# One call of a cross-attention loop moved on ScalarE: the exponential of a tile ahead of the normalisation of the tile before

## What is computed

```python
qp = ctx @ Wq.T + bq ; kp = ctx @ Wk.T + bk
scores = (qp @ kp.T) * 128**-0.5 * layernorm(x)      # 512 x 512 for each batch
scores = where(mask, -inf, scores)
x = x + softmax(scores)                              # attention step, residual
xn = layernorm(x)
shared = silu(xn @ sg) * (xn @ su) @ sd              # shared expert
logits = xn @ router_w                               # 8 experts, top 2, sigmoid
x = x + shared + sum over chosen experts of ffn_e(p_e * xn)
```

## Time and profile before

| what | value |
|---|---|
| time, median of 3 runs | 365.19 us (364.84 to 365.95) |
| the profiled execution | 365.61 us, span 363.9 us |
| busy: PE, POOL, DVE, ACT | 320.0, 231.0, 208.1, 177.6 us |
| granted TensorE clock, mean | 0.958 |

### The profile page before, as it was taken

One profiled execution on the slowest core, in us unless ns is written; L12 is line 12 of the kernel. 1 busy time (PEld: TensorE's weight loads), 2 busy tenths in 40 slices (PEclk: granted clock), 3 DMA queues, 4 the chain that ended last, 5 costly groups with the idle time before them and its releaser, 6 DMA issues.

```text
span 363.9 us, 6490 instructions
## 1 busy us (share of the span) xinstructions
PE 320.0 (88%) x1627; PEld 217.8 (60%) x1627; DVE 208.1 (57%) x461; ACT 177.6 (49%) x400; POOL 231.0 (63%) x199
## 2 busy tenths in 40 slices
PE   2857999899999994648999999999999999999991
PEld 1324666576666762315776766777777777777760
DVE  0666887898998889612444444444444444444440
ACT  2467767667757645102644434444444444444430
POOL 0688999886675739948376565656555465555433
PEclk9999999999999998556999999999999999999998
DMA  7956788746646420075346466857666666575736
GB/s 186 304 203 200 222 241 239 272 145 214 221 146 196 153 86 0 0 193 165 57 92 98 83 116 118 143 95 125 113 113 117 115 119 116 91 130 86 134 36 82
DMA packets 29763, 50.61 MB, mean 139 GB/s; under 512 B 5472, under 2 KB 9312, under 8 KB 29728
## 3 DMA queue, kind: packets, MB, share of 16 engines
q0 software_dynamic: 9008, 21.66, 33.7%
q1 hardware_dynamic: 19232, 27.99, 24.3%
q10 hardware_dynamic: 1488, 0.54, 0.7%
HBM read 30.45 MB, written 19.73 MB: 138 GB/s over the span
## 4 chain that ended last, share of the span: by engine, by line
PE 48%; POOL 19%; issue 10%; ACT 7%; DMA 7%; DVE 6%; POOLq 0%; SPq 0%; DVEq 0%; ACTq 0%
PE bank L948 9%; PE bank L958 8%; PE bank L953 8%; POOL gu_lo L356 7%; PE bank L981 5%; PE bank L987 5%; PE bank L984 5%; POOL dn_lo L356 5%; PE bank L1072 4%; DMA out_rows<-y,jscatter 3%; POOL rstd L332 3%; PE bank L967 2%; ACT gu_hi L493 2%; ACT bank L488 2%; POOL pen L351 2%
## 5 line engine op out<-in xcount | busy, mean ns | idle before, releaser
L439 POOL DMA_INDIRECT out_rows<-y,jscatter x39 | 61.9, 1588 | 73.5 <-DMA out_rows<-y,jscatter 47.9
L958 PE MATMUL bank<-gu_hi,x_lo 128*128 (+1 forms) x220 | 70.9, 444 | 0.0
L948 PE MATMUL bank<-gu_hi,x_hi 128*128 (+1 forms) x220 | 62.4, 406 | 3.4 <-POOL dn_lo L356 1.4
L953 PE MATMUL bank<-gu_lo,x_bf 128*128 (+1 forms) x220 | 57.5, 384 | 0.0
L670 DVE TENSOR_TENSOR x_lo<-bank,x_hi 128x512 fp32r<-128x512 f32 x55 | 37.7, 686 | 26.4 <-ACT x_bf L507 25.3
L863 DVE SCALAR_TENSOR_TENSOR h<-bank,xg,h 128x256 f32<-128x256 f32 x39 | 18.9, 484 | 58.4 <-ACT h L594 57.0
L420 POOL DMA_INDIRECT xg<-xn_rows,jgather x39 | 41.7, 1069 | 16.1 <-issue 15.1
L514 ACT CAST h_hi<-bank 128x256 fp32r<-128x256 f32 x55 | 20.6, 374 | 60.9 <-PE bank L967 59.0
L958 PEld LDWEIGHTS bank<-gu_hi,x_lo 128*128 128x128 f32 x220 | 42.0, 191 | 12.7 <-issue 0.3
L356 POOL TENSOR_TENSOR gu_lo<-stage,gu_hi 128x1024 bf16<-128x1024 f32 x18 | 43.4, 2412 | 9.7 <-ACT gu_hi L493 9.7
L948 PEld LDWEIGHTS bank<-gu_hi,x_hi 128*128 128x128 f32 x220 | 40.5, 190 | 13.7 <-issue 3.1
(11 more groups left out here) (128 smaller groups left out, 491.5 us busy)
## 6 DMA issues: line engine op xcount, KB each, us to landing
stage<-in_L_ffn_gate_up_w SPq DMA_DIRECT2D x16, 512.0 KB, 3.8
xin<-in_x SPq DMA_DIRECT2D x16, 256.0 KB, 4.3
xn_rows<-xn SPq DMA_DIRECT2D x16, 256.0 KB, 3.8
stage<-in_L_ffn_down_w SPq DMA_DIRECT2D x8, 512.0 KB, 3.8
out_rows<-x SPq DMA_DIRECT2D x16, 256.0 KB, 4.2
out_rows<-zeros POOLq DMA_DIRECT2D x1, 1024.0 KB, 5.0
ctx_in<-in_ctx SPq DMA_DIRECT2D x1, 768.0 KB, 8.8
xg<-xn_rows,jgather POOLq DMA_INDIRECT x39
```

The source lines that it names most:

```text
L439: g.indirect_dma_start(out=out, out_offset=bass.IndirectOffsetOnAxis(ap=jscatter[:, n - TILES:n - TILES + 1], axis=0), in_=y[:, r, :], in_ ...
L948: tn.matmul(ps_g(n)[:], x_hi[:, n % TS, k, :], gu_hi[:, e, k, :], start=(k == 0), stop=False)
L953: tn.matmul(ps_g(n)[:], x_bf[:, n % TS, k, :], gu_lo[:, e, k, :], start=False, stop=False)
L958: last = tn.matmul(ps_g(n)[:], x_lo[:, n % TS, k, :], gu_hi[:, e, k, :], start=False, stop=(k == KC - 1))
```

## The change

On ACT, normal() is called one step later: in step s the exponential of tile s comes first, then the normalisation of tile s - 1, then the rest of the step. Nothing else changes, neither the semaphores nor the other engines' lists.

```diff
@@ -547,6 +547,8 @@
             for s in range(TILES):
                 j = s - LAG
                 expo(s)
+                if s:
+                    normal(s - 1)
                 if s + 1 < B:
                     projections(s + 1)
                 if s + 2 < B:
@@ -563,7 +565,6 @@
                         chosen_exp(j)
                     if s == TILES - 2:
                         late_high(EARLY)
-                    normal(s)
 
             chosen_exp(FIRST - 1)
             h_high(FIRST - 1)
```

## The result

The changed kernel takes 363.47 us (median of 9 runs, 362.2 to 364.35) against 365.31 us before (9 runs): the ratio is 0.9942, with a 95% interval of 0.9925 to 0.9958. That is 2.1 us faster by the ratio (1.5 to 2.7), where 1.8 us was forecast.

A forecast was written before the change was run, and what follows sets the result against it. POOL was taken to set steps 1 to 6, and equal POOL-ACT and TensorE loops the later ones, TensorE limiting the gain. Terms 0.34 + 1.25 + 0.15, said as 1.8 us, gave 363.4 us against the median; range 362.7 to 364.2.

The forecast's parts named there:

- The three loops of a later step: Steps 7 to 14: ACT and POOL need 5.97 us, DVE 6.30 to 6.34, TensorE 6.68 to 6.72, the longest.
- the repeated 4.62 us: TensorE's stretch L948 to L911 takes 4.62 us in later steps and in step 7 alike, so it is work, not waiting.
- the full busy row: Later steps: the matmul engine is busy 6.72 of 6.72 us, read as TensorE having no room.
- The eight later steps: Steps 7 to 14 together gain 0 to 0.3 us, taken as 0.15, since TensorE's loop limits them.
- The join: Step 7, after POOL's pace ends: L967 starts 1.25 us earlier, won once and kept by TensorE.
- The second rival: Transposes of xn hold TensorE in steps 2 to 6, so the join wins 0.5 us or less: 364.7 us; chance 0.20.
- The first steps: Steps 1 and 2: POOL's low_part comes 0.34 us earlier (bounds 0 and 0.59); steps 3 to 6 only carry it on.
- The tail: Step 15 onward: an earlier exponential gives 0 to 0.1 us, and what is won at step 15 arrives at the first gather.
- The sum: Whole kernel: 0.34 + 1.25 + 0.15 = 1.74 us, said as 1.8 with the start of the tail.
- The slower rival: Later steps lengthen if DVE's bias comes over 0.3 us later against TensorE: 367.9 us; chance 0.09.
- One sign to watch: In the changed profile, POOL's low_part still waits, longer than before.

The follow-up runs named there:

- run 6: Changed kernel with the shared expert's low part of gate and up cut to one slice of four for tiles 0 to 13; single execution 363.23 us.
- Run 5: Kernel before (old order) with the shared expert's low part of gate and up cut to one slice of four for tiles 0 to 13; single execution 367.11 us.
- run 1: Only normal() of tiles 0 to 6 moved, the other tiles in the old place, against the kernel before: 363.44 us, ratio 0.9955.
- run 2: Only normal() of tiles 7 to 14 moved, the other tiles in the old place, against the kernel before: 365.24 us, ratio 0.9993.
- run 3: Only normal() of tiles 5 to 14 moved, the other tiles in the old place, against the kernel before: 363.21 us, ratio 0.9946.
- run 4: The full change once more, all 15 normal() calls moved, against the kernel before: 362.82 us, ratio 0.9932.
- run 7: Old order with the second weight chunks in steps 0, 1, 3, 5, 7 and 9, not 0 to 5, against the kernel before: 366.43 us, ratio 1.0025.
- Run 10: Changed kernel with DVE's x_stats ahead of neg_max, so the exponential's bias comes 0.6 us later; steps 8 to 13 took 6.76 to 6.77 us, no kernel time given.

## Why the prediction was right

*The three loops of a later step* were forecast at 5.97 us (ACT and POOL), 6.30 to 6.34 (DVE) and 6.68 to 6.72 (TensorE). The runs show each by itself: nmr(6) to nmr(7) in the changed kernel is 5.97 us; the steps of run 6 are 6.35; those of the changed kernel 6.69, with TensorE alone in the chain. Run 5 shows that the first of them was real as well. The reason I gave for TensorE (the repeated 4.62 us) holds; the full busy row that I named beside it carried nothing.

*The eight later steps*: 0 to 0.3 us, taken as 0.15; seven of them, from h(7) to h(14), gave 0.28. That is near the bound, since the part behind L967 went from 1.25 to 1.21 us every time.

*The join*: 1.25 us, measured 1.19 (nmr(6) to h(7)). Runs 1 to 3 show that normal(5) and normal(6) make it. The second rival's mechanism did set in: in steps 3 to 6 the transposes of xn now wait for the later normal. From 38 to 72 us TensorE's sequencer waits:

```profile
PEld bank L968 <- DVE h L685: 1.7, 4, 0.5
PEld bank L921 <- ACT xn L526: 1.2, 3, 0.5
```

It costs nothing at step 7, because POOL sets nmr(6) and TensorE has caught up by then. Run 3, which has the late normals in two steps only, shows the same h(7), less the start's share: nmr(6) to h(7) is 2.53 us there.

*The first steps*: 0.34 us, measured 0.33 at nmr(2). Of it 0.16 is left at nmr(6): this term was over-sized, and the sentence that failed is that steps 3 to 6 only carry it on. nmr(2) to nmr(3) took 7.46 us for 7.28: in step 3 half_tanh waited 0.19 us for TensorE's gate and up, and POOL's low_part 0.17 us for the copy behind it. In this profile, and in runs 1 and 4 (7.46, 7.43), TensorE ran at its low clock for a while about steps 2 and 3; in run 6, where it did not, the distance is 7.27 and the 0.3 us stay. But run 6 also has less work for TensorE, and no trace has the new order with the full work, the bias in its place, both chunks and the full clock there, so that the clock alone took the 0.16 us is not shown. The windows from 35 to 40 us, before and changed:

```profile
35.00:40.00 5.00, 4.76 (x29) 3.49 (x30) 3.74 (x9) 3.60 (x9) 4.49 (x5) 1.00 0.65 224
...
35.00:40.00 5.00, 4.41 (x21) 2.95 (x22) 3.71 (x10) 3.16 (x8) 4.14 (x5) 0.70 0.63 192
```

The new order alone does not bring the low clock: run 7, in the old order, has the same (0.77 in that window, 8.38 us from h to h in step 2), and run 6, in the new, has 1.00. Whether it makes it more frequent stays open: 4 of the 8 traces in which normal(0) and normal(1) are moved show it there, and 1 of the 6 in which they are not.

*The tail*: 0 to 0.1 us, measured 1.71 - 1.63 = 0.08, and what was won at step 14 arrives at the gather whole.

*The sum*: 1.8 us forecast, 1.71 in the trace at the gather (0.16 + 1.19 + 0.28 + 0.08), 2.1 (1.5 to 2.7) by the ratio of the times. The join, two thirds of it, came out as worked out. That the sum is so close is in part luck: the first steps brought 0.18 us less than their term and the later steps 0.13 us more, and the two misses cancel.

*The slower rival* was priced by 0.3 us of spare time for xn. Run 10 shows that the place was right and the price too high: with a bias 0.6 us later each later step is 0.03 us worse than in the old order, but the lead at h(7) is lost too.

*One sign to watch was wrong.* I wrote that POOL's wait before its low part would become longer. It is 8.9 us in six steps (6.4 + 2.5), against 9.9 in the same window before (7.0 + 2.9): POOL's wait is the step less POOL's own work, and the step became no longer.

## What to carry to other kernels

When two loops of a steady stage are equally long, taking a link out of one shows nothing in the step; look for the place where the stage before it hands over, and for the room that has come free, and move work into it (0.6% for the reordering alone, 1.4% with the work spread). To know whether an engine's stretch is work, compare its start-to-start distance in a step where its data were long there with one where they were not; a busy share doesn't tell. An engine that runs in order passes each wait on to all behind it: after this change the exponential's bias delays three other things, and a late bias costs more than it did.

## What the runs showed of the hardware

The granted TensorE clock fell to half (1.2 GHz, 0.5 in the rows) for a stretch between 20 and 34 us in 11 of the 14 traces, in both orders, and a second time between 36 and 42 us in 5 of these 11. Between 18 and 40 us TensorE's weight loads had single waits of up to 3.4 us in the kernel before and in run 3, whose clock never fell there, and of up to 2.8 us in the changed kernel, whose clock fell twice; what decides it stays open. Where it fell about step 2, that step took 8.4 to 8.6 us from h to h and not 6.7 to 7.8. Behind the table stage, where TensorE had waited for DVE and POOL, the clock was low in both profiles, but in the changed kernel's with a stretch at 2.4 GHz in between (0.71 to 0.78 from 149 to 170 us, against 0.50 to 0.56); at job 2 this went with 0.6 us between the two profiles, a third of the change's own gain. Over all traces the distance from the gather to job 2 ran from 11.3 us (clock 0.74 from 5.5 to 11.3 us behind the gather) to 12.7 us (0.50).
